# A batch's two score units side by side and its four value units side by side, with the key products of the next stage placed behind each group

## The reference

```
qf, kf = taylor_exp(q), taylor_exp(k)          # 1, x/2, x_i*x_j/(4*sqrt(2)): so that
A_qk = tril(einsum("bhnd,bhmd->bhnm", qf, kf)) # A = ((1 + s)^2 + 1) / 2 of the score s
y = einsum("bhnm,bhme->bhne", A_qk, v)         # 16 heads, 64 values each
y = y * rsqrt(mean(y * y, -1) + 1e-5) * g_weight
out = y @ Wo.T
```

## Time and profile before

| what | value |
|---|---|
| median of 3 runs | 1169.72 us (1168.29 to 1170.6) |
| span of the profiled execution | 1165.0 us |
| between the median and that span | 4.7 us |
| instructions | 21556 |
| TensorE busy in the span | 1001.8 us (86%) |
| stage 3, with the changed order | from about 457 us to 662 us of the span |

### The profile page before, as it was taken

The page is one execution under the profiler, slowest core; times in us unless marked ns, Lnnn a source line. Parts: engine busy times, 40 slices in busy tenths (PEclk is TensorE's granted clock), DMA queues, the critical chain, the costliest instruction groups (busy, mean ns, idle before and its releaser), DMA issues.

```text
span 1165.0 us, 21556 instructions
## 1 busy us (share of the span) xinstructions
PE 1001.8 (86%) x8624; PEld 707.4 (61%) x8624; DVE 640.4 (55%) x1519; ACT 588.3 (50%) x1374; POOL 284.6 (24%) x292
## 2 busy tenths in 40 slices
PE   7996898887689988789998799889888897789995
PEld 4664565665388854456655676667666665447654
DVE  3246545666669833454455476776676664527003
ACT  5532565552468844344544354556555544465741
POOL 2521412100500033211112202221132124132733
PEclk9988889898989999899999988999999888679998
DMA  9341464102679785422252243313222105000001
GB/s 311 99 86 40 112 127 110 45 12 98 209 272 314 259 278 168 139 88 85 80 173 88 81 120 105 101 34 107 81 57 78 27 1 226 1 1 1 1 1 32
DMA packets 66676, 123.68 MB, mean 106 GB/s; under 512 B 11632, under 2 KB 41968, under 8 KB 62496
## 3 DMA queue, kind: packets, MB, share of 16 engines
q1 hardware_dynamic: 64528, 117.48, 33.0%
q0 software_dynamic: 2048, 4.82, 1.4%
HBM read 86.30 MB, written 35.92 MB: 105 GB/s over the span
## 4 chain that ended last, share of the span: by engine, by line
PE 56%; DVE 19%; ACT 11%; DMA 5%; issue 4%; POOL 4%; SPq 1%; another core or an unknown queue 0%; DVEq 0%; ACTq 0%; POOLq 0%
PE psum L398 38%; DVE s_p L2695 3%; ACT s_p L2653 3%; POOL rs L2985 2%; PE psum L2612 2%; DVE s_max L2684 2%; PE psum L2623 2%; PE psum L1369 2%; PE psum L2784 1%; DVE s_pT L2676 1%; PE psum L550 1%; DVE s_max L653 1%; PE psum L2173 1%; PE psum L2159 1%; PE psum L2604 1%
## 5 line engine op out<-in xcount | busy, mean ns | idle before, releaser
L2653 ACT ACTIVATE s_p<-psum,s_max 112x375 f32<-112x375 f32 x128 | 72.3, 569 | 87.6 <-DVE s_max L2684 87.6
L693 POOL TENSOR_TENSOR rstd<-meanvar,minus_half 112x1 f32<-112x1 f32 x40 | 23.1, 578 | 279.6 <-DVE meanvar L645 209.9
L653 DVE TENSOR_REDUCE s_max<-psum 112x2 f32<-112x750 f32 x64 | 59.4, 935 | 32.5 <-PE psum L550 31.4
L2985 POOL TENSOR_TENSOR rs<-ms,minus_half 112x32 f32<-112x32 f32 x8 | 43.5, 5442 | 110.3 <-DVE ms L2919 110.3
L398 PE MATMUL psum<-Wv,ctx 128*125 128x512 f16 x240 | 59.6, 392 | 11.2 <-ACT s_v L624 5.4
L398 PE MATMUL psum<-ctx,Wk 128*128 128x375 f16 x320 | 62.8, 331 | 5.0 <-ACT s_yT L2242 2.8
L2684 DVE TENSOR_REDUCE s_max<-psum 112x1 f32<-112x375 f32 x128 | 63.7, 539 | 2.3 <-PE psum L2604 2.1
L2612 PE MATMUL psum<-ident,s_p 112*125 112x112 f32 x384 | 61.4, 294 | 3.9 <-DVE s_p L2695 2.3
L609 ACT ACTIVATE s_k<-psum 128x375 f16<-128x375 f32 x64 | 31.2, 488 | 62.1 <-PE psum L398 59.5
L2604 PE MATMUL psum<-s_k,s_q 64*112 64x375 f16 x384 | 46.0, 345 | 17.0 <-ACT s_p L2653 6.5
L2612 PEld LDWEIGHTS psum<-ident,s_p 112*125 112x125 f32 x384 | 51.7, 198 | 13.7 <-DVE s_p L2695 3.9
(11 more groups left out here) (360 smaller groups left out, 2445.1 us busy)
## 6 DMA issues: line engine op xcount, KB each, us to landing
keys<-s_k SPq DMA_DIRECT2D x64, 187.5 KB, 2.2
s_k<-keys SPq DMA_DIRECT2D x8, 1500.0 KB, 7.6
values<-s_v SPq DMA_DIRECT2D x48, 224.0 KB
s_v<-values SPq DMA_DIRECT2D x16, 672.0 KB
raw_wg<-in_wg SPq DMA_DIRECT2D x8, 1024.0 KB, 6.6
raw_wu<-in_wu SPq DMA_DIRECT2D x8, 1024.0 KB, 7.1
raw_wd<-in_wd SPq DMA_DIRECT2D x8, 1024.0 KB
s_kd<-k_halves SPq DMA_DIRECT2D x48, 93.8 KB, 3.8
```

The source lines that it names most:

```text
L653: VE.tensor_reduce(s1_max[b % 2][:, 2 * p:2 * p + 2], rings["s1"][unit][0:N, :, 0:S], X, ALU.max, negate=True).then_inc(*V.up("max1", n))
L2653: SC.activation(rings["p4"][2 * n + j], rings["s4"][(n, j)][0:N, 0:S], ACT.Exp, bias=s4_max[b % 2][:, h:h + 1], accum_out=s4_sum[b % 2][:, ...
L2985: GP.tensor_tensor(rs5[b % 2][:], ms5[b % 2][:], minus_half[:], ALU.pow).then_inc(*G.up("rs5", b))
```

## The change

A batch's two score units are placed in one step with nothing between them, then comes one step that yields nothing, then five that place a key product each. The four value units are placed in one step, followed by three key products (eight in each batch as before). `s3_out` gets one more wait at build time: `turn3` is placed only when a bank of `z3` has its release in the plan. No instruction is added or removed.

```
@@ s3_heads
             for r, half in ((2 * q, "half3a"), (2 * q + 1, "half3b")):
                 rings["a3"].take((b, r), (T, ("y3", b, r)))
             rings["misc3"].take(("s3b", b, q), (A, ("sq3b", b, q)))
-            yield [("s3", b, q)]
-            yield next(keys4, None)
+            place(("s3", b, q))
+        yield None
+        for _ in range(5):
             yield next(keys4, None)
         for c in range(KC):
             rings["y3"].take((b, c), (A, ("y3", b, c)))
-        for r in range(4):
-            yield [("y3", b, r)]
+        yield [("y3", b, r) for r in range(4)]
+        for _ in range(3):
             yield next(keys4, None)
@@ s3_out
             yield from until(("y3e", b, j))
             yield from rest(REST / 2)
+            yield from until_free("z3", 1)
             yield [("turn3", b, j), ("sq3", b, j)]
```

## The result

| | median us | range, runs | against the kernel before |
|---|---|---|---|
| kernel before | 1169.46 | 1168.29 to 1170.6, 4 | |
| changed kernel | 1190.44 | 1182.39 to 1198.19, 4 | 1.0157 [1.0111, 1.0203] |
| changed kernel, timed again | 1184.05 | 1179.08 to 1193.16, 4 | 1.0107 [1.0053, 1.0161] |

What follows compares the result with a forecast made beforehand. TensorE was taken to bound the kernel, busy 86% of the span, with 9.1 us idling in stage 3's body. 6.2 + 0.8 + 0.8 + 1.0 - 0.8 = 8.0 us less gave 1161.7 us, range 1156 to 1169.

Steps and rivals of the forecast that it cites:

- value units side by side: Stage 3: a run of 32 value matmuls takes 1.68 us, not 2.16, with fewer entries; 6.2 us won over eight batches.
- score units side by side: Stage 3: pairing saves 0.27 us a batch, counted for three batches only; 0.8 us won, bounds 0 and 2.2.
- idling in the body: Stage 3, 476 to 602 us: bank waits at pairs of batches 1 to 6 total 8.4 us against 9.1 before; 0.8 won.
- idling in the opening: Start of stage 3: the 2.3 us wait for a bank DVE frees late moves to a later unit; 1.0 us won.
- clock: TensorE's clock staying low for longer would move the time a few us either way; left out of the sum.
- idling in the close: End of stage 3: key products used up early leave the last batches' chains less covered; 0.8 us lost, bounds 0 and 8.
- The rival with a wait at each pair: Every score pair in stage 3 takes its own bank again, 3.7 us each; about 1183 us, chance 0.12.
- The one with no denser runs: Stage 3: a run of matmuls takes as long as the same in pieces; 1 to 2 us won, 1168, chance 0.10.
- banks stop mattering: Stage 3: the new order drops every present `yT3` wait, nearly 20 us less at best; about 1154, chance 0.10.
- comes earlier, where TensorE has no gap, so the sum is unchanged: Some 13 key products, 10 us of TensorE's work, leave stage 3's last two batches for earlier places without loss.
- the other edits cost nothing by themselves: Stage 3: the `turn3` build-time wait and closer key products are free; one 2.2 us ACT store wait is in the range.
- the rival at 1168: Close of stage 3 laid bare: the last two batches, without key products, give back 6 to 8 us; chance 0.15.

Runs made afterwards that it cites:

- e3: Kernel before with only the value units side by side, plus the new build-time wait; 1184.99 us, 1.0156 to the kernel before.
- e2: Kernel before with only the score units side by side, plus the new build-time wait; 1185.81 us, 1.0165 to the kernel before.
- the control: Kernel before with the new build-time wait alone, unit order unchanged; 1174.12 us, 1.0046 to the kernel before; its stage 3 took 202.7 us.
- e4: Changed kernel with stage 4's first loads placed later, behind the score units of batch 6; 1179.68 us, 1.0076 to the kernel before.
- e6: Kernel before with value units side by side, heads' steps kept at 16 a batch, and the new build-time wait; 1179.96 us, 1.0047 to the kernel before.
- e8: Changed kernel without key products as filler in `weave`; 1177.26 us, 1.0060 to the kernel before.
- e9: Kernel before with 40 useless small ACT copies ahead of batch 3's value copy; 1175.79 us, 1.0032 to the kernel before.
- e15: Kernel before with 64 useless small ACT copies ahead of batch 3's value copy; 1177.32 us, 1.0038 to the kernel before.
- e14: Changed kernel with 70 useless matmuls in four gaps, at batches 3 and 5 and in the close; 1176.31 us, 1.0036 to the kernel before.

## Why the prediction was wrong

| term | forecast, us | measured, us |
|---|---|---|
| value units side by side | 6.2 won | 6.4 won (e3) |
| score units side by side | 0.8 won | 2.4 won (e2) |
| both, as work at the high clock | 7.0 won | 10.1 won |
| idling in the body (9.1 before) | 0.8 won | 2.7 lost |
| idling in the opening (4.2 before) | 1.0 won | 0.4 lost |
| idling in the close (9.1 before) | 0.8 lost | 11.1 lost |
| clock | no part of the sum | 10.7 lost, 6.6 against the control |
| stage 3 | 8.0 won | 14.8 lost (12.8 against the control) |

The idling is each window's length less TensorE's busy time: 11.8 in the body, 4.6 in the opening, 20.2 in the close.

**Right: the packing.** The run of 32 value matmuls takes 1.68 us from 531.72 to 533.40, as forecast. The scores gave more than counted, as told below. "TensorEngine Tiling (Array Packing)" of the Trainium skill, section Key Properties, says that different tiles can work in parallel. The trace agrees: at 650.10 the 16 matmuls of two score units take 1.04 us, where the 8 of one take 0.94.

**Right: what a pair waits for.** The gaps at the pairs of batches 1 to 6 are 0.81, 0.21, 2.10, 1.00, 3.62 and 1.04 us, 8.8 in all, where 0.7, 0.7, 2.3, 0.5, 3.7 and 0.5 were forecast, 8.4 in all. As idling these waits are right; that those of batch 5 would also bring 6.8 us of low clock was not seen. The rival with a wait at each pair (1183 us) thus gave nearly the right time for the wrong reason. The one with no denser runs is out by e2 and e3; that banks stop mattering, by the waits for `s_a`. The rule of the Trainium skill that emptying PSUM may become the bottleneck ("TensorEngine Tiling (Array Packing)", section Performance Considerations, under PSUM Bottleneck) is not borne out as a mean, with DVE and ACT busy for 102 and 85 of 215 us, and holds only just behind the pairs: TensorE's waits for `s_a` in the rows shown are 4.2 + 2.5 = 6.7 us, forecast at 6 to 10.

**The step that failed first: "comes earlier, where TensorE has no gap, so the sum is unchanged"**, and with it "the other edits cost nothing by themselves". I counted 0.8 us for the whole of it in the close, and the close lost 11.1. My walk through the plan had found the four or five fillers in a row and the heads' waiting for `scale3`. Where the fillers go I looked at TensorE alone, and held their coming early for free. But each is also an ACT copy, a DVE copy and a store, in a ring of four buffers, and ahead of batch 6 the stores met the loads of stage 4's first keys and values. The wait of 2.2 us that I kept "in the range" came twice, 2.96 and 3.29, and carried over to `scale3` through DVE's queue: 6.8 us. The copies of the burst ahead of batch 4 made another 1.9, with no store in the chain longer than 2.26. In both places I had `scale3` "ahead of it anyway". That it is ahead in the plan says nothing of the chip. e4 shows the link; e6 and e8 show that with the weaving kept, or without fillers, most of the loss goes. e2, which lost as much with no burst at all, shows that this step is not the whole. The rest of the close (3.3 us behind a norm, 3.7 behind the last `scale3`) is the chain laid bare, the rival at 1168: true, and too small.

**The step that failed second: the clock as "no part of the sum".** I named it as something that could prove me wrong by "a few us either way". It cost 10.7 us (6.6 against the control). It can only go one way where the row before says 0.99 or 1.00, and a forecast with a gap of several us in it has to price that. e9 and e15 show that the gap makes the low clock, e14 that filling the gaps brings it back. "TensorE: Matmul & The Clock Gate" of the Trainium skill, sections "HAM oscillation — how this bites in real kernels" and "A second HAM failure mode: psum-queue depth-cycling", tells of kernels whose clock goes back and forth when TensorE keeps waiting, for a DMA or for PSUM banks, and of the work behind the wait then running slow. The trace agrees: the clock is 0.69 in the 22 us about the wait that a store began, and ten key products behind it take 3.32 us in place of 1.76.

**Two slips in the sums.** By its own terms the rival where banks stop mattering gives about 1156 us and not 1154, and 9.1 less 8.4 is 0.7. Neither changes the argument.

**What stays open.** How the loss splits between the two steps, since low clock also lengthens chains that TensorE then waits for. Why gaps of 1.0 to 1.6 us bring low clock in some executions and not in others, with the same order. And why stretches with the same order ahead of stage 3 took 461.0 to 478.1 us in these traces: this moves the total by more than the change in some runs, and is why a stage was compared here, and not the span alone.

## What to carry to other kernels

Before you pull work together, ask of all that gets moved with it which buffers, which queue and which DMAs it needs at its new place: a filler is free on the engine that has a gap only if it is free on the ones that empty it. Where a stage runs at a clock of 1.00 with gaps of about 1 us, price a new gap of several us twice, once as idling and once as slower work behind it. And if two parts of a change each cost as much alone as both together, look in each one's trace before you name a common cause: they shared the order of the plan here, but one lost by stores and the other by waits for banks.

## What was not expected of the hardware

- Two score units back to back can take little more than one. The 8 matmuls of one took 0.94 us on two row groups; 16 take 1.04 in the changed kernel at 650.10, where those of all four row groups start within 0.04 us of each other. At 477.70 and 506.77 the second unit started only behind the first, and the 16 took 1.77, within the 1.7 to 1.9 that was forecast. That the banks were free in one case and not in the other is argued from the order of the waits.
- The clock falls for a gap that an ordinary wait makes. Behind 3.51 us of idling came 3.4 us at 1.2 GHz, behind 5.75 us 6.8, behind 6.77 with 1.04 to follow 13.7; behind single gaps of about 1.0 us, well apart, none. In the longer two it begins inside the gap: the 13.7 us start at 633.8, and the gap ends at 638.23. Behind gaps of 1.48 us and less at one pair, the same order had none in two executions and 13.7 us in two others.
- The store of one key product took 9.07 us from DVE's end to ACT's release where the DMA engines were busy with loads and stores for 0.95 of the 10 us from 620, at 272 GB/s; the median of the stores from 612 to 640 us was 2.7 us from issue to landing.
